# Queries and keys of two attention layers computed by features, 512 tokens moving, with rows brought to the operands by DMA

## What is computed

```python
x = x + 0.5 * ffn0(layernorm(x))          # x W^T + low rank, scaled per output feature
x = x + attn0(layernorm(x))               # 32 query heads, 8 key heads of 16, rotated, causal
x = x + 0.5 * ffn0(layernorm(x))
x = x + 0.5 * moe1(layernorm(x))          # base product, 8 experts of rank 16, best 2
x = x + attn1(layernorm(x))               # 8 heads of 32, causal
x = x + 0.5 * moe1(layernorm(x))
```

## Time and profile before

| | |
|---|---|
| median of 3 runs | 1405.7 us (1405.19 to 1406.45) |
| the profiled execution | 1411.57 us, span 1409.8 us |
| mean granted clock of TensorE, share of full speed | 0.929 |
| busy, of the span | TensorE 91%, weight loads 58%, VectorE 67%, ACT 45%, POOL 34% |
| DMA | 39.60 MB, mean 28 GB/s |

### The profile page before, as it was taken

One profiled execution on the slowest core, in us unless ns is written; L12 is line 12 of the kernel. 1 busy time (PEld: TensorE's weight loads), 2 busy tenths in 40 slices (PEclk: granted clock), 3 DMA queues, 4 the chain that ended last, 5 costly groups with the idle time before them and its releaser, 6 DMA issues.

```text
span 1409.8 us, 21535 instructions
## 1 busy us (share of the span) xinstructions
PE 1286.9 (91%) x7392; PEld 824.5 (58%) x7392; DVE 943.4 (67%) x2782; ACT 639.8 (45%) x959; POOL 483.3 (34%) x733
## 2 busy tenths in 40 slices
PE   3988999999899998998979889999998999999988
PEld 1886543444268896444858854444432788954368
DVE  5664888999337944652857468889991587366356
ACT  1236266666632335444212544666665222544522
POOL 1574031221155542114626621321122554311162
PEclk9999588999999999899989976999999999989999
DMA  9200000001002001000140000000010100010001
GB/s 300 92 1 30 2 2 2 32 3 40 1 1 71 1 1 39 2 2 0 61 145 1 1 31 2 2 4 31 2 40 2 57 16 1 3 37 1 2 0 60
DMA packets 19420, 39.60 MB, mean 28 GB/s; under 512 B 4401, under 2 KB 5681, under 8 KB 19185
## 3 DMA queue, kind: packets, MB, share of 16 engines
q1 hardware_dynamic: 19312, 38.23, 8.0%
HBM read 32.33 MB, written 11.29 MB: 31 GB/s over the span
## 4 chain that ended last, share of the span: by engine, by line
PE 69%; DVE 16%; POOL 5%; issue 4%; ACT 4%; DMA 2%; SPq 0%; DVEq 0%; ACTq 0%; POOLq 0%
PE bank L781 16%; PE bank L674 12%; PE bank L596 8%; PE bank L598 7%; PE bank L597 7%; DVE maxes L980 5%; PE bank L765 4%; PE bank L654 4%; PE bank L759 3%; PE bank L576 3%; DVE unused L976 3%; PE bank L684 2%; POOL probs L1254 1%; DVE xT L844 1%; DVE gate L904 1%
## 5 line engine op out<-in xcount | busy, mean ns | idle before, releaser
L1180 ACT ACTIVATE probs<-bank 128x1024 f32<-128x1024 f32 (+3 forms) x416 | 367.9, 911 | 304.3 <-PE bank L765 195.6
L674 PE MATMUL bank<-ops 48*128 48x512 f32 (+3 forms) x960 | 321.0, 438 | 13.2 <-DVE maxes L980 3.8
L976 DVE CUSTOM_DVE_ANT_0 unused<-bank,causal 128x128 bf16<-128x128 f32 (+3 forms) x640 | 279.5, 486 | 73.9 <-PE bank L674 70.5
L1333 POOL TENSOR_SCALAR_AFFINE_SELECT probs<-probs 128x256 f32<-128x256 f32 (+1 forms) x256 | 118.8, 464 | 590.1 <-ACT probs L1180 589.9
L674 PEld LDWEIGHTS bank<-ops 48*128 48x128 f32 (+1 forms) x960 | 162.5, 207 | 198.2 <-DVE maxes L976 81.6
L781 PE MATMUL bank<-probs,v_mem 128*17 128x512 f32 (+6 forms) x1920 | 259.1, 531 | 6.1 <-ACT heads_raw L1169 5.6
L980 DVE TENSOR_REDUCE maxes<-bank 128x1 f32<-128x512 f32 x320 | 207.2, 684 | 38.0 <-PE bank L674 36.4
L1080 ACT CAST xT<-bank 128x512 fp32r<-128x512 f32 (+1 forms) x128 | 71.3, 560 | 280.5 <-PE bank L576 280.5
L844 DVE TENSOR_TENSOR xT<-bank,xT 128x512 fp32r<-128x512 f32 (+1 forms) x128 | 83.6, 656 | 148.4 <-ACT xT L1080 148.4
L765 PE MATMUL bank<-ops 50*128 50x512 f32 (+2 forms) x640 | 177.9, 454 | 4.1 <-ACT probs L1180 4.0
L596 PE MATMUL bank<-w_odd_hi,xT 128*128 128x384 f32 (+2 forms) x448 | 169.0, 377 | 2.1 <-DVE xT L844 1.9
(11 more groups left out here) (102 smaller groups left out, 1743.6 us busy)
## 6 DMA issues: line engine op xcount, KB each, us to landing
w_odd_lo<-staging_wqkv SPq DMA_DIRECT2D x4, 1536.0 KB, 6.7
x<-x_dram SPq DMA_DIRECT2D x16, 256.0 KB, 6.0
out_dram<-x SPq DMA_DIRECT2D x16, 256.0 KB, 2.0
staging_wqkv<-wqkv_dram SPq DMA_DIRECT2D x2, 1536.0 KB, 14.1
ops<-staging_dora SPq DMA_DIRECT2D x3, 1024.0 KB, 5.1
ops<-staging_base SPq DMA_DIRECT2D x2, 1296.0 KB, 6.4
w_odd_lo<-staging_base SPq DMA_DIRECT2D x2, 1296.0 KB, 5.8
ops<-shiftT SPq DMA_DIRECT2D x160, 4.0 KB
```

The source lines that it names most:

```text
L674: last = mm(dst[:, h * w:(h + 1) * w], queries(a, u)[rows, t // 4, hi, t % 4 * P:(t % 4 + 1) * P], keys(a, u, hi)[rows, HALF * kp:HALF * k ...
L976: V.tensor_tensor_reduce(unused[:, masked % 3, 0:w], part, causal[:, HALF - w:], 1.0, NEG, ALU.add, ALU.max, dst).then_inc(s["max_done"].s ...
L1180: A.activation(probs[:, e % 6, :, 0:cols], scores[:, 2 * (e % 2):2 * (e % 2) + 2, 0:cols], ACT.Exp, scale=a.scale).then_inc(s["exp"].sem, 1)
L1333: G.affine_select(out=p, in_=p, compare_op=ALU.is_ge, fill=0.0, base=0, pattern=pattern, channel_multiplier=-1).then_inc(s["masked"].sem, 1)
```

## The change

Queries and keys are computed transposed: for QK features the weights are stationary (128 features) and 512 tokens of the turned x move, so that a product (j, g) gives feature block j for tokens 512 g to 512 g + 511 directly in the operands' layout. The stacks, their transposes and the copies of these go. The values are still computed by tokens, in two groups of four tiles. The order of the products is written out in `plan_products`; three PSUM banks serve them in turn.

In `QKV0` the features are ordered so that a rotation's two parts stand in two products on the same partitions. VectorE multiplies each product, bias added, by cosine and sine (`heads_read`), `rope_sums` adds (on VectorE for the first four sets, on POOL for the last two), ACT writes high parts (`rope_high`), POOL low parts (`rope_low`), and SP stores both in DRAM (`store_rope`, six DMAs a set) and loads them as rows of the operands (`load_keys`, `load_queries`). The query block of heads 16 to 31 is rotated in the chain, its parts are made and stored in the first unit of attention, and query operands of unit u + 3 are loaded when unit u has been scored. In `QKV1` ACT writes the high part of each of a product's four heads straight to its 32 operand rows, VectorE the low part, and one DMA copies the high part to its second place (`copy_high`).

The chains are now ticks (`plan_chain`): a tick has turns, a product of a plain stage or products of heads. The turns of `QKV0` begin four ticks before `FFN_A` ends, those of `QKV1` three ticks before `MOE_A`'s turns end, so that two tiles are turned in each of these ticks. VectorE's epilogue stands first in an iteration: for plain stages that of the product one tick before, for experts that of the product two ticks before. `hw` is transposed into a bank of its own. The split of `WO1`'s weights moves into the attention. The constant rows of ones come by DMA (`load_ones`).

```diff
+    def plan_products(self):
+        first, second = [("v", t) for t in range(4)], [("v", t) for t in range(4, NT)]
+        if self.rope:
+            order = [(0, 0), (1, 0), (2, 0), first, (0, 1), (1, 1), (2, 1), (3, 0), (4, 0), (3, 1), (4, 1), second]
+            self.begun = {8: 3, 9: 6, 10: 9, 11: 12}
+        else:
+            order = [(0, 0), (1, 0), first, (3, 0), (0, 1), (1, 1), (3, 1), second, (2, 1), (2, 0)]
+            self.begun = {5: 2, 6: 4, 7: 6, 8: 9, 9: 12}
...
+def plan_chain(chain):
+    plain = [(st, t) for st in chain if st not in ATT for t in range(NT)]
+    ticks = [Tick([it], plain[n - 1] if n else None) for n, it in enumerate(plain)] + [Tick([], plain[-1])]
+    if chain[-1] in ATT:
+        st, a = chain[-1], ATT[chain[-1]]
+        early = len(plain) - (3 if chain[-2] in MOE_RANK else 4)
+        ticks += [Tick([], None, p) for p in a.ticks]
+        for t in range(NT):
+            ticks[early + t].turns.append((st, t))
...
+            def heads_product(b, st, kind, j, g=0, between=None):
+                dst = qkv_banks[m % 3]
+                pe.wait_ge(xT_ready.sem, xT_ready.at(b, TURN_NO[st, 4 * g + 3 if kind == "qk" else j] + 1))
...
+                    pe.wait_ge(s["read"].sem, s["read"].at(b, m - 2))
...
+                    for k in range(KC):
+                        mm(dst, hi[:, k, cols], x_hi[:, k, :], start=(k == 0), stop=False)
+                        mm(dst, lo[:, k, cols], x_hi[:, k, :], start=False, stop=False)
+                        last = mm(dst, hi[:, k, cols], x_lo[:, k, :], start=False, stop=(k == KC - 1))
...
-            def turn_piece(b, st, t, n):
...
+            def heads_read(b, st, kind, j, g=0):
...
+                    for first, lanes in pieces:
+                        for i, table in enumerate((cos, sin)):
+                            last = V.scalar_tensor_tensor(prods[0:lanes.stop - lanes.start, first + i, :], src[lanes, :],
+                                                          bias_qk0[lanes, j:j + 1], table[lanes, :], ALU.add, ALU.mult)
+                    last.then_inc(s["read"].sem, 1)
+                    if (j, g) in ropes and n < 4:
+                        rope_sums(dve, V, b, n)
+                else:
+                    dve.wait_ge(s["hi"].sem, s["hi"].at(b, sum(p[0] == "qk" for p in a.products[:m + 1])))
+                    for h in range(4):
+                        hi, lo = head_rows1(j, h, g)
+                        last = V.scalar_tensor_tensor(lo, src[32 * h:32 * (h + 1), :], bias_head1[:, 4 * j + h:4 * j + h + 1],
+                                                      hi.bitcast(F32), ALU.add, ALU.subtract)
...
+            def chain(b, c):
+                    before = [ticks[i - n].product if 0 <= i - n < len(ticks) else None for n in (1, 2)]
+                    if before[1] is not None and before[1][0] in MOE_RANK:
+                        epilogue(b, *before[1])
+                    if before[0] is not None and before[0][0] not in MOE_RANK:
+                        epilogue(b, *before[0])
+                    for it in tick.turns:
+                        turned_lo(b, *it)
+                    for it in ticks[i + 2].turns if i + 2 < len(ticks) else ():
+                        statistics(b, *it)
+                    if experts:
+                        routing(b, *tick.product)
+                    for it in ticks[i + 1].turns if i + 1 < len(ticks) else ():
+                        normalise(b, *it)
+                    if experts:
+                        weigh(b, *tick.product)
...
+            def rotated_operands(b):
+                for g in range(2):
+                    store_rope(b, 2 * g)
+                    store_rope(b, 2 * g + 1)
+                    load_keys(b, g)
+                    load_queries(b, 0, g)
...
+                rotated_operands(b)
                 after(b, QKV0)
+                for u in (1, 2):
+                    load_queries(b, u, 0)
+                    load_queries(b, u, 1)
                 load_weights(b, WO0)
-                attention(b, QKV0)
+                rotated_attention(b)
```

More of the change, by code:

```diff
@@ L442, in build @@
         block = ctx.enter_context(nc.Block())
-        items = [[(st, t) for st in chain for t in range(NT)] for chain in CHAINS]
+        ropes = [(0, 0), (2, 0), (0, 1), (2, 1), (4, 0), (4, 1)]
+        rope_lanes = [64, P, 64, P, P, P]
         @block.sync
@@ L508, in stage, with standard_attention @@
+            def standard_attention(b):
+                for u in range(A1.units):
+                    load_shifts(b, QKV1, u, 0)
+                    load_shifts(b, QKV1, u, 1)
             def stage(name):
@@ L604, in product @@
+            def product(b, st, t):
                 n = begin(b, st, t)
@@ L1005, in shift_parts @@
+            def attention(b, st):
+                for i in range(max(ATT[st].begun.values()), ATT[st].ring_len):
+                    ring_read(b, st, i)
             def shift_parts(b, st, u, c):
@@ new lines, in heads_high @@
+            def heads_high(b, j, g):
+                a, s = A1, qs[QKV1]
+                m = a.product_no("qk", j, g)
+                if m == 0 and b == 0:
+                    act.wait_ge(s_qkv_bias, 16 * 5)
+                act.wait_ge(s["product"].sem, s["product"].at(b, m + 1))
+                for h in range(4):
+                    hi, _ = head_rows1(j, h, g)
+                    last = A.activation(hi, qkv_banks[m % 3][32 * h:32 * (h + 1), :], ACT.Identity,
+                                        bias=bias_qk1[32 * h:32 * (h + 1), j:j + 1])
+                last.then_inc(s["hi"].sem, 1)
@@ L1144, in chain @@
+            def chain(b, c):
+                ticks, att = TICKS[c], ATT_OF_CHAIN.get(c)
+                for i, tick in enumerate(ticks):
+                    for st, t in tick.turns:
+                        copy_turned(b, st, t)
                         nb, nst = (b, st + 1) if st < MOE_B else (b + 1, FFN_A)
-                        if nb < BATCH and nst != WO0 and 2 <= t < 2 + chunks_of[nst]:
+                        if nb < BATCH and nst not in WO_ATT and 2 <= t < 2 + chunks_of[nst]:
                             split_chunk(nb, nst, t - 2)
-                    if 2 <= i < len(its) + 2 and its[i - 2][0] in MOE_RANK:
-                        copy_hw(b, *its[i - 2])
@@ L1149, in chain @@
-                    if 5 <= i < len(its) + 5 and its[i - 5][0] in ATT:
-                        for n in range(ATT[its[i - 5][0]].pieces):
-                            evacuate(b, *its[i - 5], n)
-                    if 1 <= i < len(its) + 1 and its[i - 1][0] in MOE_RANK:
-                        gate_exp(b, *its[i - 1])
-                    if 3 <= i < len(its) + 3 and its[i - 3][0] in ATT:
-                        high_parts(b, *its[i - 3])
+                    before = ticks[i - 1] if i else Tick()
@@ new lines, in chain @@
+                    if before.product is not None and before.product[0] in MOE_RANK:
+                        copy_hw(b, *before.product)
+                    if tick.product is not None and tick.product[0] in MOE_RANK:
+                        gate_exp(b, *tick.product)
+                    if att == QKV0:
+                        for p in before.heads:
+                            if p[1:] in ropes and ropes.index(p[1:]) < 4:
+                                rope_high(b, ropes.index(p[1:]))
+                    if att == QKV1:
+                        for p in tick.heads:
+                            if p[0] == "qk":
+                                heads_high(b, *p[1:])
@@ L1302, in chain @@
+            def chain(b, c):
+                ticks, att = TICKS[c], ATT_OF_CHAIN.get(c)
+                for tick in ticks[0:2]:
+                    for it in tick.turns:
+                        rstd_of(b, *it)
+                for i, tick in enumerate(ticks):
+                    for it in ticks[i + 2].turns if i + 2 < len(ticks) else ():
+                        rstd_of(b, *it)
+                    for st, t in tick.turns:
                         nb, nst = (b, st + 1) if st < MOE_B else (b + 1, FFN_A)
-                        if nb < BATCH and nst != WO0 and 2 <= t < 2 + chunks_of[nst]:
+                        if nb < BATCH and nst not in WO_ATT and 2 <= t < 2 + chunks_of[nst]:
```

842 lines of the change are left out of this document (455 added, 387 removed).

## The result

The changed kernel takes 1392.1 us (median; 1390.7 to 1395.6), the kernel before beside it 1406.1: a ratio of 0.989 (95% interval 0.985 to 0.9925). I had forecast 1350, within 1322 to 1390. It is faster, as forecast, but by 14 us and not by 56; by the profiled spans 20.5 (1409.8 to 1389.3). Two slow executions among the experiments, of e7 (1416.1 us) and e10 (2415.4 us), are left out of the ratios.

The account below looks back on a forecast made before the run. TensorE work that the change removes was taken to bound the QKV stages, and VectorE, held up by POOL, the expert stages. 7.6 - 66 + 19.1 - 16.8 = -56.1 us; off 1405.7 that gave 1350, range 1322 to 1390.

Parts of the forecast that it names:

- What goes, and products: QKV stages: 576 piece transposes go, 52 us of TensorE; products, 33.6 us before, take 33.5, moving 512 columns gaining nothing.
- Expert ticks: Expert stages: the moved epilogue and two tiles turned in a tick add 15 + 4.1 = 19.1 us.
- QKV1: Standard QKV stage: first score after 57.5 us, for 65.9 before: 2 x 8.4 = 16.8 us less.
- T': The first tick of QKV1, from which the forecast's times in that stage count.
- QKV0: Rotated QKV stage: first score at T+52, from 84.9 and 85.2 before: 2 x 33 = 66 us less.
- T: The tick of product (0,0) in QKV0, from which the forecast's times in that stage count.
- the cover of the rows: QKV0: row stores and loads by DMA hidden with 5 us of cover, except shift rows 1 to 2 us late.
- FFN_A: Last feed-forward ticks: with two tiles turned VectorE takes 4.4 us in a tick of 3.4; +3.8 us a batch, +7.6.
- A: Expert stages: the epilogue's order is neutral, the sum loses its 19.1 us, 1331 us; chance 0.13.
- B: QKV0's rows by DMA come late: 6 us a batch, 1362 us, or some 25, 1400 us; chance 0.14.
- C: QKV product ticks: TensorE at half clock, slower than before, up to 134 us more, 1450 at three quarters; chance 0.10.
- D: QKV0: held by VectorE and its maxima, removed transposes only turn into waits; no change, 1405 us; chance 0.03.

Follow-up runs that it names:

- e7: The changed kernel with QKV0's turns beginning two ticks before the end of FFN_A, not four: 1401.3 us, 0.994.
- e10: e6 with VectorE's two gate operations of 8 elements comparing logits in PSUM instead of expert numbers in SBUF: 1341.4 us, 0.953.
- e1: The changed kernel with the expert tile's epilogue back between the norm and the gates, one tick behind its product: 1375.5 us, 0.978.
- e3: The changed kernel with ScalarE signalling each head's high part in QKV1, so VectorE need not wait for all four: 1375.9 us, 0.976.
- e4: The changed kernel with SyncE sending unit 0's shift rows before unit 2's query rows and WO0's weights: 1391.9 us, 0.9865.
- e6: The changed kernel with the edits of e1, e3, e4 and e8 together: 1347.1 us, 0.957.
- e8: The changed kernel with ScalarE copying both turned tiles before it splits weights, VectorE's order untouched: 1387.7 us, 0.986.
- e12: The kernel before with only the gate operations' source changed, logits in PSUM instead of expert numbers in SBUF: 1404.5 us, 0.997.
- e2: The changed kernel with ScalarE's split behind both copies and VectorE's norm ahead of the statistics in ticks without experts: 1388.6 us, 0.986.
- e5: The kernel before with only the expert tile's epilogue moved behind the gates, where the next iteration begins: 1443.9 us, 1.0255.

## Why the prediction was wrong, step by step

**What goes, and products.** Right: TensorE is busy 22.5 us less in QKV0 by the two windows, transposes and moved turns together, and 512 columns are one per 0.23 us in L793 to L795 as in the earlier trace rows. The Trainium skill (TensorE: Matmul & The Clock Gate, Back-to-back issue gap) gives about 131 ns; I had set it aside by that row, and it doesn't show here either. The score stretches stayed within 3 us, as forecast; the reads from PSUM with a per-partition bias take 0.67 us from start to start in QKV0 and 0.76 in QKV1, where I had 0.6.

**Expert ticks.** This is the step that failed in kind. I priced the epilogue's new place by the operations put ahead of others (0.7 us a split tick, 2 x 2.8 + 3.2 + 0.9 = 9.7 us in all) and named the queue behind it, but didn't follow it round: TensorE's first half, 1.84 us at the full clock and up to 2.9, lies in the same circle, which has no slack against TensorE's 5.0. Measured 21.7 us (e1). The two tiles turned in one tick I had at 2 x 4.75 us in the first expert stages, and e1 leaves 8.4 there.

**QKV1.** Mis-sized. ScalarE's piece of 32 partitions takes 0.69 us and VectorE's 0.76 from start to start, where I took 0.55 and 0.6 from operations of 128 partitions and no bias: 5.8 us behind each product for 4.6. (0,0) was read at T'+9.1 for 7.9 and TensorE's stop was 4.69 for 3.4. Behind it stand three more stops, 3.41, 3.28 and 2.56 us in batch 0, in which the ring waits for VectorE while VectorE works through reads of products; (2,1) was read at T'+52.4 for 45. The second stop:

```profile
509.42 9.16 DVE L1147 SCALAR_TENSOR_TENSOR ops<-bank,bias_head,ops 32x512 fp32r<-32x512 f32 x12 [4.31 <-ACT ops L1356]
519.17 0.44 PE L860 MATMUL bank<-ops 96*128 96x384 f32 x1 [3.41 <-DVE maxes L1204]
```

With the hand-off of e3 the first three are 2.61, 1.75 and 1.20 us, and the stage takes less than the forecast 57.5.

**QKV0.** The larger part came (54.5 us of 66), with three terms off (T+58.7 and T+55.8 for 52); the dearest is the cover of the rows, which I had as hidden but for 1 to 2 us. Batch 1 reads without the clock's part: all products done at T+42.2 for 40, the 12th bank read at T+45.7 for 43, the first score 2.35 us late for the shift rows where I had 1. Batch 0 has the wait of 0.84 us, and a product at the lower of the two clock levels, behind the 2.25 us stop for the turn of tile 7 (1.7 forecast): one matmul per 0.43 us, so that turn and product take 4.8 us where batch 1, behind a stop of 2.18, keeps the full clock and has 3.3.

```profile
80.16 0.63 PE L793 MATMUL bank<-ops,w_odd 128*128 128x512 f32 x1
80.58 0.63 PE L794 MATMUL bank<-ops,w_odd 128*128 128x512 f32 x1
```

With the shift rows first (e4) 5.3 us of the 10.5 too many go; with the copies in better order too (e6) it takes 53.2 and 52.8.

**FFN_A.** I summed VectorE's operations, 4.4 us. Its waits for ScalarE's copies belong in the tick as well (0.31 and 0.53 us), and the split between the copies: 5.34, or 4.72 without the split.

**Rivals.** A is out: the expert order alone costs 21.7 us. B came about in small: 5.6 us of waits for rows. C showed in short stretches only: the product above, and in QKV1 of batch 0 the matmuls behind the stops of 4.69 and 3.41 us, at a granted clock of 0.50 (0.21 us apart where 0.12 is usual, some 2.9 us in all for 2.5 forecast). D fell: QKV0 kept most of its gain. Its reason, VectorE, became the limit in the ticks around instead. The four mendable places together (e6) give 1347.1, close to the 1350 of the forecast. That is luck: e1 takes out a move that the forecast had priced at 9.7 us, e3 overlaps pieces that it had one after the other, and e8's edit was no part of the change I costed.

## What to carry to other kernels

An operation moved behind another on its queue must be followed round the whole circle of engines back to itself; the circle's sum is the new tick. Price traffic that the change adds against the engines with that traffic on them, not as the trace of before has them. Where one engine hands pieces to another, signal each piece: here that was worth 15 us by stages, for an edit of a few lines. And a small VectorE operation on the path is safe from POOL here when one of its tensors lies in PSUM (e10, e12).

## What the runs showed of the hardware

**POOL holds some of VectorE's operations, and only some.** Those with a tensor in PSUM don't stretch beside POOL in these traces (L1138 0.74 us, L1051 0.69, with POOL busy or not), nor do the statistics (0.68). Those with all tensors in SBUF can, beside a POOL operation of 1.3 us or more: the norm (0.54 us alone, up to 2.05 in the changed kernel and 2.12 in e2), the gate operations (0.28 and 0.23 alone, up to 1.76 and 1.19) and a sum of two SBUF tensors:

```profile
96.36 2.40 POOL L1476 TENSOR_TENSOR ops<-features,ops 64x1024 fp32r<-64x1024 f32 x1 [6.41 <-ACT ops L1346]
97.98 1.32 DVE L520 TENSOR_TENSOR features<-features 128x512 f32<-128x512 f32 x1
```

L520 takes 0.68 us otherwise. The Trainium skill (GPSIMD Engine Reference, Specifications) says that POOL shares its SBUF interfaces with VectorE's instructions that have two SBUF inputs or run in a two-port mode; e10 and e12 agree, down to operations of 8 elements; no run shows which of the two conditions the gate operations meet.

**The same attention takes 239 to 251 us with the granted clock.** Both rotated attentions of e1, same instructions, columns as before:

```profile
126.80:378.00 251.20, 240.91 (x1512) 99.86 (x1512) 196.43 (x664) 155.23 (x182) 56.72 (x103) 0.86 0.15 40
804.30:1043.50 239.20, 226.22 (x1512) 96.00 (x1512) 195.93 (x664) 154.82 (x181) 56.58 (x103) 0.93 0.16 42
```

In most kernels here the sum of the two is near 487 us (e1 490, e5 492, e7 494, e4 499), and nothing in the edits explains which is which. That stays open, and it is why edits worth 3 to 6 us were read by their stages.
